# A column of variances instead of a wide row in the join, and scattered cells moved between blocks

## The reference, cut to what matters

```
xn = layernorm(x)
x  = x + L0_gnn(xn, src, dst) + L0_mix(xn)      # segment max over the edges of a node
x  = x + L0_ffn(layernorm(x))                   # 8 experts, weighted by a softmax gate
xn = layernorm(x)
x  = x + L1_gnn(xn, edge_index) + L1_mix(xn)    # mean over the neighbours, three times
x  = x + L1_ffn(layernorm(x))
```

## Time and profile before

| | us |
|---|---|
| median of 3 runs | 2259.45 (2256.13 to 2262.32) |
| the profiled execution's own time | 2258.26 |
| its span in the profile | 2256.5 |
| busy in the span: PE, DVE, POOL, ACT | 1740.6, 1320.1, 1122.8, 598.0 |
| cells placed by POOL (L715), 400 of them | 524.5 |

### The profile page before, as it was taken

How to read it: one execution, slowest core, us unless ns; L and a number is a source line. 1 busy time by engine, 2 the same in 40 slices (tenths; PEclk the granted TensorE clock), 3 DMA queues, 4 the chain that set the end, 5 groups by cost and what they waited for, 6 DMA issues and landing times. The chain is left out here.

```text
span 2256.5 us, 25514 instructions
## 1 busy us (share of the span) xinstructions
PE 1740.6 (77%) x8349; PEld 1011.8 (45%) x8349; DVE 1320.1 (59%) x2672; ACT 598.0 (27%) x940; POOL 1122.8 (50%) x888
## 2 busy tenths in 40 slices
PE   7984645544553658999999628699989999996996
PEld 6962222211222434555555427555565555544543
DVE  6877866776674666777777515445541221125996
ACT  4001101110110135666666312211220010003453
POOL 0868888888885737888888768400000000000344
PEclk9557877777775669999999858799999999997998
DMA  6346788878886202111220200344325433431002
GB/s 173 85 134 195 212 225 230 216 216 219 217 215 163 54 10 61 35 34 34 34 34 9 67 1 2 52 103 109 100 50 130 124 95 92 127 80 38 0 4 82
DMA packets 193283, 229.05 MB, mean 102 GB/s; under 512 B 66688, under 2 KB 174292, under 8 KB 187811
## 3 DMA queue, kind: packets, MB, share of 16 engines
q1 hardware_dynamic: 126001, 172.58, 29.0%
q0 software_dynamic: 67200, 55.46, 11.1%
HBM read 148.81 MB, written 78.24 MB: 101 GB/s over the span
## 5 line engine op out<-in xcount | busy, mean ns | idle before, releaser
L715 POOL DMA_INDIRECT adjacency<-all_cell_val,all_cell_idx x400 | 524.5, 1311 | 173.5 <-issue 121.0
L281 POOL DMA_INDIRECT edge_ring<-b_rows,all_src_idx x400 | 494.8, 1237 | 187.0 <-issue 168.1
L1742 POOL TENSOR_TENSOR ffn_hl<-ffn_hid,ffn_hh 128x448 f16<-128x448 f32 x56 | 70.1, 1254 | 717.3 <-ACT ffn_hid L1759 717.1
L1555 PE MATMUL bank<-sage_adj,sage_zh 125*128 125x448 f16 x1050 | 370.1, 352 | 3.4 <-DVE sage_zl L1609 3.4
L1555 PE MATMUL bank<-sage_adj,sage_zl 125*128 125x448 f16 x1050 | 370.0, 352 | 0.0
L535 DVE SCALAR_TENSOR_TENSOR edge_ring<-edge_ring,w_keep 125x256 f32<-125x256 f32 x399 | 193.0, 484 | 128.6 <-DMA edge_ring<-b_rows,all_src_idx 112.8
L1201 ACT ACTIVATE bank<-bank,w_shift,w_scale 128x448 f32<-128x448 f32 x224 | 147.1, 697 | 76.7 <-PE bank L728 76.7
L1632 DVE TENSOR_TENSOR sage_u<-bank,w_rd 128x448 f32<-128x448 f32 x42 | 26.2, 625 | 236.2 <-PE bank L1560 233.4
L1555 PEld LDWEIGHTS bank<-sage_adj,sage_zh 125*128 125x128 f16 x1050 | 102.6, 98 | 101.9 <-issue 8.0
L1555 PEld LDWEIGHTS bank<-sage_adj,sage_zl 125*128 125x128 f16 x1050 | 102.7, 98 | 99.6 <-issue 5.8
L690 DVE SCALAR_TENSOR_TENSOR edge_junk<-bank,all_key_c,all_later 125x400 f16<-125x400 f32 x232 | 145.7, 628 | 0.0
(11 more groups left out here) (433 smaller groups left out, 3448.3 us busy)
## 6 DMA issues: line engine op xcount, KB each, us to landing
sage_adj<-adjacency SPq DMA_DIRECT2D x105, 490.0 KB
run_max<-edge_ring SPq DMA_DIRECT2D x40, 1120.0 KB
adjacency<-edge_zero SPq DMA_DIRECT2D x25, 714.0 KB
experts_gb<-gate_rows SPq DMA_DIRECT2D x56, 224.0 KB, 3.3
edge_ring<-b_rows,all_src_idx POOLq DMA_INDIRECT x400, 7.1
adjacency<-all_cell_val,all_cell_idx POOLq DMA_INDIRECT x400, 2.6
sage_adj<-adjacency SPq DMA_DIRECT2D x105, 56.9 KB
run_max<-edge_ring SPq DMA_DIRECT2D x40, 130.0 KB
```

The lines of the kernel that those rows point to most:

```text
L281: nc.gpsimd.indirect_dma_start(ring[:, k % RING, :], None, dram.rows[:, :], bass.IndirectOffsetOnAxis(ap=c.src_idx[:, k:k + 1], axis=0)).t ...
L715: nc.gpsimd.indirect_dma_start(dram.adj_flat, bass.IndirectOffsetOnAxis(ap=c.cell_idx[:, k:k + 1], axis=0), c.cell_val[:, k:k + 1], None). ...
L1555: ins = mm(ps[4 * b + h][:, 0:T], z[:, g * JG + j, half(h)], adj[g][:, j, :], start=(g == 0 and j == 0 and z is zh), stop=False)
L1742: nc.gpsimd.tensor_tensor(hl[:, m, :], hid[:, m, :], hh[:, m, :], ALU.subtract).then_inc(low, 1)
```

## The change

In the join, the variance of a group is made with the squares as weights and one column of `mean_w` as the moving operand, so that it comes out as 125 nodes by one column for each piece. Root and reciprocal are taken of 125x4 in SBUF tiles with two slots, and PE transposes each column, spread over 128 columns, into bank 4. The scaling waits for that (`rs_spread`) instead of for the reciprocal. In PE's list the new transposes come after the first two carry products and before the transposes of `m`. The ranges of cells become 0 to 55 (join), 56 to 297 (experts), 298 to 355 (norm2), 356 to 399 (mix1): 56, 242, 58 and 44 columns instead of 46, 244, 45 and 65.

```diff
-JOINED = 46
+JOINED = 56
@@ join_norm_gate
+        sd, rs = s.sb("sd", [B, 2, 4]), s.sb("rs", [B, 2, 4])
@@ ACT
-                        if g >= 1:
-                            act.wait_ge(scaled, g)
-                        nc.scalar.activation(ps[4][:, 0:wide(g)], ps[3][:, 0:wide(g)], ACT.Sqrt, bias=c.eps5[:, 0:1]).then_inc(sd_ready, 1)
+                        if g >= 2:
+                            act.wait_ge(rs_ready, g - 1)
+                        nc.scalar.activation(sd[:, g % 2, 0:size(g)], ps[3][0:B, 0:size(g)], ACT.Sqrt, bias=c.eps5[0:B, 0:1]).then_inc(sd_ready, 1)
@@ DVE
                         dve.wait_ge(sd_ready, g + 1)
-                        v.reciprocal(ps[4][:, 0:wide(g)], ps[4][:, 0:wide(g)]).then_inc(rs_ready, 1)
+                        if g >= 2:
+                            dve.wait_ge(rs_spread, g - 1)
+                        v.reciprocal(rs[:, g % 2, 0:size(g)], sd[:, g % 2, 0:size(g)]).then_inc(rs_ready, 1)
...
-                        dve.wait_ge(rs_ready, g + 1)
+                        dve.wait_ge(rs_spread, g + 1)
@@ PE, before the transposes of m
+                    if t >= 3:
+                        g = t - 3
+                        pe.wait_ge(rs_ready, g + 1)
+                        if g >= 1:
+                            pe.wait_ge(scaled, g)
+                        for j in range(size(g)):
+                            ins = nc.tensor.transpose(ps[4][:, B * j:B * (j + 1)], rs[:, g % 2, j:j + 1].to_broadcast([B, P]), c.ident[0:B, 0:B])
+                        ins.then_inc(rs_spread, 1)
@@ PE, the variance
-                        product(nc, ps[3][:, 0:wide(g)], [c.mean_w[:]] * KH, [sq[:, k, 0:wide(g)] for k in range(KH)]).then_inc(var_done, 1)
+                        for j in range(size(g)):
+                            ins = product(nc, ps[3][0:B, j:j + 1], [sq[:, k, B * j:B * (j + 1)] for k in range(KH)], [c.mean_w[:, 0:1]] * KH)
+                        ins.then_inc(var_done, 1)
@@ build
-            experts(nc, c, w, dram, made, lambda pool: place_cells(nc, c, dram, pool, JOINED, 290, made))
+            experts(nc, c, w, dram, made, lambda pool: place_cells(nc, c, dram, pool, JOINED, 298, made))
-                norm(nc, c, 2, lambda pool: place_cells(nc, c, dram, pool, 290, 335), [
+                norm(nc, c, 2, lambda pool: place_cells(nc, c, dram, pool, 298, 356), [
-            mix1(nc, c, w, qT, ctx, lambda pool: place_cells(nc, c, dram, pool, 335, L))
+            mix1(nc, c, w, qT, ctx, lambda pool: place_cells(nc, c, dram, pool, 356, L))
```

More of the change, by code:

```diff
@@ L894, in join_norm_gate @@
         mean_done, centred, sq_ready, var_done = s.sem("mean_done"), s.sem("centred"), s.sem("sq_ready"), s.sem("var_done")
-        sd_ready, rs_ready, scaled = s.sem("sd_ready"), s.sem("rs_ready"), s.sem("scaled")
+        sd_ready, rs_ready, rs_spread, scaled = s.sem("sd_ready"), s.sem("rs_ready"), s.sem("rs_spread"), s.sem("scaled")
         high, lowed, logits = s.sem("y_high"), s.sem("y_low"), s.sem("logits")
```

## The result

The kernel after takes 2249.73 us (median of 5 runs, 2248.46 to 2252.55), the kernel before 2259.79 (2256.13 to 2262.32, also 5). The ratio is 0.9954, 95% interval 0.9944 to 0.9965: 10.1 us or 0.46% faster. I had said 2248.8, 10.6 us less. The total came out, but not all of its terms did. The profiled execution took 2252.55 us, 5.7 less than the 2258.26 of before and not 10.6 less; it is the slowest of the five.

| block, first event to first event, us | before | after | change | forecast |
|---|---|---|---|---|
| join (first gather to first cell after it) | 155.3 | 142.8 | -12.6 | -19.1 |
| experts | 407.9 | 407.2 | -0.8 | 0 |
| norm2 and weight split | 79.4 | 98.3 | +18.9 | +19.4 |
| mix1 (to the first DMA of sage) | 107.0 | 95.1 | -11.9 | -10.9 |
| all the rest, front and back | 1506.8 | 1507.5 | +0.7 | 0 |

A forecast was written before the change was run, and what follows sets the result against it. A loop of dependences was taken to bound the join, PE the experts block, POOL the ends of norm2 and mix1. Join -19.1, experts 0, norm2 +19.4, mix1 -10.9 gave -10.6 us: 2248.8 us, range 2242 to 2256.5.

The forecast's parts named there:

- The reciprocal: Join: 125x4 takes 0.178 us where 128x500 took 3.285, 3.1 us less in each of six turns.
- The root: Join: 0.25 instead of 0.65 us, 0.4 us less where the root is waited for.
- The transposes of rs: Join, PE: about 1.1 us, free in turns 3 to 6, on the path in turn 8, about 0.5 in turn 9.
- The ten cells in the join: Join, POOL: 39 cells instead of 29 after the gather, ending at 825.6, hidden with 4 us to spare.
- Experts: Experts block: 242 cells instead of 244; compute ends the block, so 0 us.
- Norm2: Norm2 block: 58 cells instead of 45 where POOL ends the block, 13 x 1.49 = 19.4 us more.
- POOL's end in mix1: Mix1: with 21 cells fewer POOL's part falls by 31 us and ends near 1410.
- mix1: Mix1 block: 44 cells instead of 65; compute ends it, with 3.0 us of hand-over, 10.9 us less.
- the term for the variance: Join, PE: 16 one-column matmuls for 4 wide ones cost nothing to 1.5 us a turn; taken as nothing.
- rival B: Join: PE no longer reaches the higher clock; join saves 12 instead of 19 us, total 2256; chance 0.18.
- rival A: Join: PE keeps the higher clock, join saves 23 us, total 2245; chance 0.13.

The follow-up runs named there:

- e4: Kernel before, ranges and wide variance kept, reciprocal taken of 4 columns only, so scaling uses values that are not the reciprocal: 2236.82 us, ratio 0.9901.
- e2: Kernel before with only the new ranges of cells (56, 242, 58, 44), the join as before: 2270.78 us, ratio 1.0049.
- e1_join_only: Kernel after with the old ranges of cells (46, 244, 45, 65), so only the join changed: 2242.53 us, once more 2244.81.
- e5: e1_join_only plus the old wide variance product, unread, issued just ahead of the one-column products: 2246.11 us, ratio 0.9942.
- e6: e1_join_only plus one matmul, unread, behind the transposes of rs in PE's idle stretch: 2235.64 us, ratio 0.9901.
- e12: e9 with cells dealt 49, 247, 43, 61 instead of 53, 245, 43, 59: 2223.38 us, ratio 0.9852.
- e9: e1_join_only with PE's mean product moved behind variance and carry products, and cells dealt 53, 245, 43, 59: 2228.07 us, ratio 0.9863.

## Why the prediction was right, and where it was not

**Right, by its rows.** The reciprocal (0.18 us): e4 saves 22.1 us in the join by it, 19.4 by my sum. The root: 0.26 us for 0.25. The transposes of rs: free in turns 3 to 6, and on the path in turn 8 by 1.19 us and in turn 9 by 0.56, where I had said 1.2 and 0.5. The ten cells in the join: POOL ended at 825.19, forecast 825.6. Experts: -0.8. Norm2: +18.9 for 19.4. POOL's end in mix1: 1409.91 for "near 1410". The experts block started at 838.93, inside the 828 to 840 beyond which I had called the prediction wrong.

**Right by chance: mix1.** It changed by -11.9 for -10.9, but by other parts. From the first cell to the end of DVE it took 94.0 us, 0.9 more than the 93.1 of before, and the hand-over was 1.1 us, not 3.0. My 3.0 came from the ends of other blocks, as seen by POOL and ACT. In e2, with the same ranges, compute took 99.2 us and the block changed by only -6.7.

**Wrong: the term for the variance.** The step is "I take nothing: PE rises during the mean product before it, which is not touched". The one row that I took it from, is true, but it does not hold for every turn before. In turn 3 the mean ran at the lower clock to its end, and the rise came only within the wide variance, which took 2.25 us; its window is at 0.62:

```profile
751.22 3.68 PE L765 MATMUL bank<-all_xT,all_mean_w 128*128 128x500 f32 x4
...
754.70 2.25 PE L765 MATMUL bank<-join_sq,all_mean_w 128*128 128x500 f32 x4
```

In the profiled execution of the kernel after PE stayed at 0.50 from 740 to 800, and of the six variances of four columns four took 3.36 us, one 2.24 and the first, in turn 2, 1.80. The one of 2.24, in turn 6, shows that the clock can rise within such columns too; mostly it did not. The periods between reciprocals (turn 3 to 4, and so on, from their start times) show where it fell, in us:

| turns | 3-4 | 4-5 | 5-6 | 6-7 | 7-8 | 8-9 |
|---|---|---|---|---|---|---|
| before | 18.09 | 17.58 | 16.74 | 16.68 | 14.31 | 9.62 |
| after | 17.13 | 17.13 | 15.11 | 13.53 | 10.62 | 7.37 |
| saved | 0.96 | 0.45 | 1.63 | 3.15 | 3.69 | 2.25 |
| forecast | 3.1 | 3.1 | 3.5 | 3.5 | 3.3 | 2.3 |

The last three are right. In the first three 6.7 us are missing, and the rows account for them: from turn 4 to 5 the variance took 3.36 for 1.84 us, the mean 3.68 for 3.54, and the six carry products behind them, which I had only in rival B's price and there at 0.5, 3.00 for 1.88: 2.8 us of the 2.65 missing. From 3 to 4 it was 1.1 in the variance and 1.5 in eight carry products, for 2.1 missing; from 5 to 6 it was 1.5 in the variance and 0.4 in the mean, for 1.9. That is rival B's mechanism, at 12.6 us saved for its 12. I gave it 0.18 and should have given it at least as much as the forecast: the mix1 row showed a stretch in which such products did not raise the clock, and I used it only against rival A.

**Why the total still fits.** The profiled execution is 5.7 us faster than that of before, not 10.6. The clock in the join is not the same in each execution: that of e1_join_only lasted 133.7 us in one and 142.6 in another, and my forecast lies between. Over five runs the kernel after has a median 2.8 us below its profiled run, and that of before 1.5 us above its own: 5.7 + 2.8 + 1.5 = 10.0. So that the median came out within 1 us of the forecast is in part luck. The mean granted clock of a whole run, on record for each, was 0.843 and 0.844 in the two runs of 2252 us and 0.847 to 0.849 in the three of 2248 to 2250, so turns with the higher clock may well come back in some runs; that they are those of the join is not shown. How often they come back in the kernel after can't be said from one profile, and e1, e4 and e5 too have runs 7 to 11 us apart; that stays open.

The rule of the Trainium skill that I weighed ("TensorE: Matmul & The Clock Gate", section "HAM oscillation — how this bites in real kernels": gaps bring PE down, shorter gaps leave it high) forecast rival A. The gap did shrink, from 6.87 us to 0.57 and 1.70, and the clock sank; in e5, with the wide product back and all the rest as in e1, it rose. So the gap alone did not decide here. That it has no part is not shown: e6, which fills part of it, had more high windows than e1.

## What to carry to other kernels

The one-column form of this product costs what the wide one does at either level of the clock (3.36 us for the 3.68 of a product as wide at the lower, 1.80 for 1.84 at the higher), yet with it PE can lose the higher level for these columns and for what follows; so price such a change at both levels, and don't assume that the level of before stays. In a loop of dependences first look at the order in the in-order queue: moving a product that nobody in the loop waits for behind the one that all wait for gave 8 us in the join of the kernel before, and 14 us of median together with what the clock gave back. That is about as much as the 9 us between the best and the usual clock. Set the ranges of filler work by where its engine idles before the barrier, and count what that engine's instructions cost beside the other engines' bursts.

## What the runs showed of the hardware that I had not expected

- Of one kernel, two executions differ by 9 us in one block through PE's granted clock alone (0.63 and 0.58, join 133.7 and 142.6 us). The Trainium skill ("TensorE: Matmul & The Clock Gate", section "What's actually happening") says that the point of the rise shifts from run to run; here it decides over whole turns.
- An indirect DMA on POOL that takes 1.19 us took up to 6.90 beside an unbroken burst of DVE instructions (e12), and 4.33 beside a single one of 3.49 us (before).
- How long a block's end takes depends on which engine ends it and which one is looked at. After POOL ended a block, its own next cell came 4.9 us later in the join (e9, e12) and 4.4 after the experts block (e12), where the 3.1 from norm2 was to ACT's first instruction. After DVE ended mix1 in the kernel after, SP's first DMA came 1.1 us later.
